# A graph network's isomorphism layer: where the second bias is added and which engine reads the product from PSUM

## The chip, the cores and the metric

The kernel runs on one core of a Trainium2 chip. The metric is the device time of one execution in microseconds (us). The kernel before takes 5115.66 us, the median of 3 runs (5112.63 to 5118.18).

## The reference

Four graph layers follow one another over 100,000 nodes of 64 features and 50,000 edges sorted by destination; each is followed by a residual add and a layer norm. The change touches only the third, the isomorphism layer, which is, for the node table `x` (100,000 x 64):

```
agg = segment_sum(x[src], dst)
h   = relu((x + agg) @ W1 + b1) @ W2 + b2
x   = layernorm(x + (x + relu(h)))
```

W1 and W2 are 64 x 64, b1 and b2 have 64 numbers, all of it in float32.

## The kernel before

The program is a row of passes, one per layer or half layer, each closed by a barrier of all engines: `Sage0`, `Sage1`, `Sage2`, `Gcn1`, `Gcn2`, `Gin` (the isomorphism layer), `Messages`, `Update`. A pass walks over 50 blocks m of 2048 nodes (16 tiles of 128). A block is worked in two groups q = 0, 1 of 8 tiles, so that most operations are instructions of 128 x 512 float32 that come in pairs.

In `Gin` a block goes through these steps; the letters in brackets are the semaphore that each raises.

- GpSimd gathers the source rows of the block's edges, 8 indirect DMAs of 128 rows (`gather_pool`, L678), up to three blocks ahead; it may fill the ring only behind the sums of an older block (`agg0`, `agg1`).
- SyncE copies the gathered rows into three shifted rings, 9 DMAs (`skewed`, L1041), three blocks ahead. The same queue loads the node rows (L864, `load_b`), stores the result (L966) and loads the kept one-hot matrices as bytes (L1103, `bytes`). In one turn m it does, in this order: next index list in every fourth turn (L870); wait for `pre0`, `pre1`, then load_b of m+2; the 9 copies of m+3; wait for `out0`, `out1`, then the store of m; the bytes of m+4. The index list of a turn thus stands right behind the bytes of the turn before.
- TensorE turn m (`tensor`): turn the inputs round (L1225, 8 transposes) once VectorE has made them (`mean`); sums of group 0 of m+1 with one-hot matrices (L749); first product with W1 (L1621); sums of group 1 of m+1; second product with W2 (L1231, 8 matmuls of 128 columns, PSUM banks 6 and 7, `mm`), once ScalarE has made its input (`relu`). In the profile each float32 matmul is two records.
- VectorE turn m (`vector`): inputs of m+1 (`take`, L1550); product plus bias row from PSUM to SBUF (L1559, `sum`); 2x + relu (L1562, `pre`, waits for `last`); row sums, means and centring (L780, L785, L789, `xc`); sums of the squares (L829, `vs`); 1/root (L837) and the result into `store_a` (L843, `out`).
- ScalarE turn m (`scalar`): relu of that sum, SBUF to SBUF (L1598, `last`); turned inputs of m+1 out of PSUM (L1575, `ev`); bytes of m+3 widened to float32 for group 0 (L1128, waits for the DMA of the bytes, `hot0`); squares of m (L810, `sq`); hidden layer of m+1 (L1583, `relu`); roots (L815, `sd`); bytes of m+3 for group 1 (L1128).

The order on each engine is written out by hand; a wait holds up all that stands behind it on its engine.

Of the kernel before, what the change touches and what calls it, by code (L numbers as in the profile page):

```python
# [23 lines left out]
F32, BF16, I32, U8 = mybir.dt.float32, mybir.dt.bfloat16, mybir.dt.int32, mybir.dt.uint8  # L24
ALU = mybir.AluOpType
ACT = mybir.ActivationFunctionType
AX = mybir.AxisListType

P = 128
NT = 16  # L30
BN = P * NT
GT = 8
ET = 8
HT = 4
D = 64
# [28 lines left out]
def build(nc, z, a, out):  # L64
# [5 lines left out]
    def sb(name, shape, dt=F32):  # L70
        return ctx.enter_context(nc.sbuf_tensor(name, shape, dt))
# [14 lines left out]
    def kept(name):  # L86

        return f"{name}_{current[0]}" if name[0:2] == "g_" else name

    def S(name):  # L90
        if name in POOL_DMAS:
            key = kept(name)
            if key not in soft:
                soft[key] = ctx.enter_context(nc.semaphore(key))
            return soft[key]
        if name not in names:
            names[name] = sets[current[0]][len(names)]
        return names[name]
# [28 lines left out]
    def now(uses):  # L127

        return uses + (1 + first[0])

    def before(uses):

        return uses + first[0]
# [20 lines left out]
    def block_of(table, m, width):  # L154
# [20 lines left out]
    wg1, wg2, wi1, wi2 = (sb(n, [P, P]) for n in ("wg1", "wg2", "wi1", "wi2"))  # L175
# [5 lines left out]
    b1r, b2r, bg2r, bi2r, bm2r, bu2r = (  # L181
        sb(n, [P, w]) for n, w in (("b1r", H), ("b2r", D), ("bg2r", D), ("bi2r", D), ("bm2r", D), ("bu2r", D)))
# [3 lines left out]
    ps = [ps_all[:, 512 * i:512 * (i + 1)] for i in range(8)]  # L186

    def work(name, bytes_):
        return sb(name, [P, bytes_ // 4])
# [11 lines left out]
    store_b = [work(f"store_b{u}", NT * H * 4) for u in range(2)]  # L201
    tmp = [[work(f"tmp{k}{q}", 2048) for q in range(2)] for k in range(2)]
    tp = [work(f"tp{q}", 2048) for q in range(2)]
    tq = [work(f"tq{q}", 2048) for q in range(2)]
    stat = sb("stat", [P, 2, 6, GT])
    bytes8 = [sb(f"bytes8_{u}", [P, 2 * HOT], U8) for u in range(2)]
    sq = [work(f"sq{q}", 2048) for q in range(2)]
    ix_now = sb("ix_now", [P, 2 * IX], I32)
    ix_dst = sb("ix_dst", [P, 2 * IX], I32)

# [412 lines left out]
    def bodies(eng, body, by=2, behind=2):  # L623


        n = (NB - behind) // by
        with eng.Fori(0, n) as it:
            for v in range(by):
                body(it * by + v, it * (by // 2) + v // 2, v % 2)
        for m in range(n * by, NB):  # L630
            body(m, m // 2, m % 2)
# [17 lines left out]
    def later(m, i, u):  # L649
        return m + 1, i + u, 1 - u  # L650
# [102 lines left out]
    def group(ap, q, W=D):  # L753

        return ap[:, q * GT * W:(q + 1) * GT * W]

    def tiles3(ap, W=D):
        return ap.rearrange("p (j w) -> p j w", w=W)
# [5 lines left out]
    def row(b, W=D, n=GT):  # L764

        return b[:, :].unsqueeze(1).to_broadcast([P, n, W])
# [8 lines left out]
    def norm_center(ve, m, pre, act_groups=()):  # L775

        V = nc.vector
        for q in range(2):
            ve.wait_ge(S(f"pre{q}"), now(m))
            V.tensor_reduce(stat[:, q, 0, :], tiles3(pre(q)), AX.X, ALU.add).then_inc(S(f"rs{q}"), 1)  # L780
        for q in range(2):
            ve.wait_ge(S(f"rs{q}"), now(m))
            if q in act_groups:
                ve.wait_ge(S(f"shift{q}"), before(m))
            V.tensor_scalar(stat[:, q, 1, :], stat[:, q, 0, :], -1.0 / D, None, ALU.mult).then_inc(S(f"nm{q}"), 1)  # L785
        for q in range(2):
            if q not in act_groups:
                ve.wait_ge(S(f"nm{q}"), now(m))
                V.tensor_tensor(tiles3(tmp[0][q][:, :]), tiles3(pre(q)),  # L789
                                stat[:, q, 1, :].unsqueeze(2).to_broadcast([P, GT, D]), ALU.add).then_inc(S(f"xc{q}"), 1)  # L790
# [40 lines left out]
    def norm_out(ve, m, to, act_groups=()):  # L831
        V = nc.vector
        for q in range(2):
            ve.wait_ge(S(f"sd{q}"), now(m))
            if q in act_groups:
                ve.wait_ge(S(f"out{q}"), before(m))
            V.reciprocal(stat[:, q, 4, :], stat[:, q, 3, :]).then_inc(S(f"rstd{q}"), 1)  # L837
        for q in range(2):
            ve.wait_ge(S(f"rstd{q}"), now(m))
            if q in act_groups:  # L840
                V.tensor_tensor(stat[:, q, 5, :], stat[:, q, 1, :], stat[:, q, 4, :], ALU.mult).then_inc(S(f"shift{q}"), 1)
            else:
                V.tensor_tensor(tiles3(group(to, q)), tiles3(tmp[0][q][:, :]),  # L843
                                stat[:, q, 4, :].unsqueeze(2).to_broadcast([P, GT, D]), ALU.mult).then_inc(S(f"out{q}"), 1)

    class Pass:
# [308 lines left out]
        def vector_loop(self, ve, windows):  # L1155
            for m in range(self.ahead - 1):
                self.hots(ve, m, m, windows)
            self.take_block(ve, 0, 0, 0, windows)
            self.hots(ve, self.ahead - 1, (self.ahead - 1) % 2, windows)
            bodies(ve, lambda m, i, u: self.vector(ve, m, i, u, windows), by=TURN if windows else 2)  # L1160
# [62 lines left out]
    def pair_transposes(pe, src, bank):  # L1223
        for r in range(GT // 2):
            last = pe.transpose(bank[:, r * P:(r + 1) * P], src[:, r * P:(r + 1) * P], ident[:, :])  # L1225
        return last

    def pair_products(pe, lhs, w, bank):

        for r in range(GT // 2):  # L1230
            last = pe.matmul(bank[:, r * P:(r + 1) * P], lhs[:, r * P:(r + 1) * P], w[:, :], start=True, stop=True)  # L1231
        return last

    class Sage2(Pass):
# [228 lines left out]
    class Gcn2(Pass):  # L1463
# [14 lines left out]
        def pre(self, u):  # L1478
            return lambda q: (tmp[1], tq)[u][q][:, :]
# [56 lines left out]
    class Gin(Pass):  # L1536
# [15 lines left out]
        def vector(self, ve, m, i, u, windows):  # L1552
            V = nc.vector
            for q in range(2):
                self.take(ve, *later(m, i, u), q, windows)
            for q in range(2):
                ve.wait_ge(S(f"mm{q}"), now(m))
                ve.wait_ge(S(f"out{q}"), before(m))
                V.tensor_tensor(tiles3(tmp[0][q][:, :]), tiles3(ps[6 + q]), row(bi2r), ALU.add).then_inc(S(f"sum{q}"), 1)  # L1559
            for q in range(2):  # L1560
                ve.wait_ge(S(f"last{q}"), now(m))
                V.scalar_tensor_tensor(tmp[1][q][:, :], group(load_b[u], q), 2.0, tmp[1][q][:, :], ALU.mult, ALU.add).then_inc(S(f"pre{q}"), 1)  # L1562
            norm_center(ve, m, pre_of)
            self.hots_ahead(ve, m, u, windows)
            norm_var(ve, m)
            self.stored(ve, i, u)
            norm_out(ve, m, store_a[u])

        def turned(self, act, m):
            if not exists(m):  # L1570
# [23 lines left out]

        def scalar(self, act, m, i, u, windows):
            for q in range(2):
                act.wait_ge(S(f"sum{q}"), now(m))
                nc.scalar.activation(tmp[1][q][:, :], tmp[0][q][:, :], ACT.Relu).then_inc(S(f"last{q}"), 1)  # L1598
            ahead = m + 3, i + 1 + u, 1 - u
            self.turned(act, m + 1)  # L1600
            self.widen_group(act, *ahead, 0, windows)
            for q in range(2):
                norm_square(act, m, q, pre_of)
            self.bent(act, m + 1)
            norm_root(act, m)
            self.widen_group(act, *ahead, 1, windows)

        def tensor(self, pe, m, i, u, windows):
            if windows:
                places = self.places(m + 1, 0)  # L1610
            for q in range(2):
                pe.wait_ge(S(f"mean{q}"), now(m))
                pe.wait_ge(S(f"ev{q}"), before(m))
                pair_transposes(pe, load_a[q], ps[2 + q]).then_inc(S(f"tr{q}"), 1)
            if windows:
                self.collect(pe, *later(m, i, u), 0, places)
                places = self.places(m + 1, 1)
            for q in range(2):
                pe.wait_ge(S(f"ev{q}"), now(m))
                pe.wait_ge(S(f"relu{q}"), before(m))  # L1620
                pe.matmul(ps[4 + q], wi1[:, :], tp[q][:, :], start=True, stop=True).then_inc(S(f"hid{q}"), 1)  # L1621
            if windows:
                self.collect(pe, *later(m, i, u), 1, places)
            for q in range(2):
                pe.wait_ge(S(f"relu{q}"), now(m))
                pe.wait_ge(S(f"sum{q}"), before(m))
                pair_products(pe, tq[q], wi2, ps[6 + q]).then_inc(S(f"mm{q}"), 1)


    CT = 4  # L1630
# [912 lines left out]
```

## Time and profile before

| | |
|---|---|
| median of 3 runs | 5115.66 us |
| span of the profiled execution, first to last instruction | 5104.4 us |
| mean granted TensorE clock, whole program | 0.937 of full |
| `Gin`, first take to last store | 3419 to 3975 us |
| TensorE, VectorE, ScalarE, GpSimd busy, whole span | 82%, 65%, 54%, 64% |

The profiled execution is told by its span; the work around it has no row of its own, and the span stands 11.3 us below the median of the timed runs. In the timelines a row is: start us, duration us, engine, line, operation, out<-in, how many merged, and in brackets the idle time just before it with what ended it. SPq rows are DMAs as SyncE issues them, not as they move. In the rows by line: busy us and mean ns of one, then the idle time of the engine just before the group.

### The profile page before, as it was taken

To read this page: it belongs to the slowest core of one execution; us is meant where nothing else is said; L and a number is where in the kernel's file an instruction comes from. 1 tells how busy PE (TensorE), PEld (TensorE's weight loads), DVE (VectorE), ACT (ScalarE), POOL (GpSimd) and SP (SyncE) were. 2 spreads that over 40 slices of the span, in tenths; PEclk is the share of its full clock that TensorE was granted. 3 is DMA by queue.
4 is the path that set the end of the run, shared out by engine and by line. 5 is a ranking of instruction groups with operands and counts; after the bars stand their busy time and mean duration, and the time that the engine had idled before them with its cause. 6 is when DMAs were issued, how large, how long until landed. Compare 5 with 4: busy or idle time off the path is not lost. (4 is left out here: it accounts for less than half of the span.)

```text
span 5104.4 us, 115936 instructions
## 1 busy us (share of the span) xinstructions
PE 4188.4 (82%) x31393; PEld 3787.4 (74%) x31394; DVE 3326.6 (65%) x6783; ACT 2761.8 (54%) x7100; POOL 3288.9 (64%) x3162
## 2 busy tenths in 40 slices
PE   2999999799997899979997455548878599999997
PEld 1899999799997898879997454536667366666666
DVE  5555555677775788857676666758888355555555
ACT  0566666455554778754443566656666244444444
POOL 2544443578773777747775777747775677777772
PEclk9999999899999999989999767779999799999999
DMA  1677777466665678758876566657776244444442
GB/s 35 213 252 252 253 251 245 173 233 241 232 235 209 223 258 264 258 198 276 280 265 222 163 186 186 186 148 214 219 210 201 73 121 117 116 117 118 117 115 90
DMA packets 490326, 991.05 MB, mean 194 GB/s; under 512 B 156821, under 2 KB 246965, under 8 KB 470968
## 3 DMA queue, kind: packets, MB, share of 16 engines
q1 hardware_dynamic: 389368, 872.44, 50.6%
q0 software_dynamic: 100800, 116.72, 10.9%
q8 instruction: 72, 1.18, 0.1%
q14 instruction: 86, 0.70, 0.0%
HBM read 452.18 MB, written 380.15 MB: 163 GB/s over the span
## 5 line engine op out<-in xcount | busy, mean ns | idle before, releaser
L749 PE MATMUL ps_all<-arena 128*128 x16000 | 2028.0, 286 | 500.5 <-DMA arena<-arena 365.3
L749 PEld LDWEIGHTS ps_all<-arena 128*128 128x128 f32 x16000 | 1993.3, 204 | 549.1 <-issue 544.7
L678 POOL DMA_INDIRECT arena<-n_t,ix_now x784 | 905.1, 1154 | 429.5 <-issue 404.7
L678 POOL DMA_INDIRECT arena<-y_t,ix_now x784 | 808.3, 1031 | 349.8 <-issue 331.9
L1128 ACT ACTIVATE arena<-bytes 128x2048 f32<-128x2048 uint8 (+1 forms) x300 | 475.9, 1618 | 299.6 <-DMA bytes<-pairs_d 209.2
L678 POOL DMA_INDIRECT arena<-x_rows,ix_now x392 | 373.1, 952 | 375.4 <-PE ps_all L749 263.4
L1639 PE MATMUL ps_all<-w,tp 128*128 128x128 f32 x4000 | 490.9, 276 | 28.8 <-ACT store_b L1782 28.2
L1639 PEld LDWEIGHTS ps_all<-w,tp 128*128 128x128 f32 x4000 | 477.9, 192 | 47.2 <-issue 38.6
L678 POOL DMA_INDIRECT arena<-x_t,ix_now x392 | 385.9, 985 | 191.4 <-issue 172.0
L708 DVE TENSOR_TENSOR arena<-iota,window 128x1024 f32<-128x1024 f32 x302 | 363.4, 1219 | 100.8 <-ACT bytes L1093 93.9
L1093 ACT ACTIVATE bytes<-arena 128x1024 uint8<-128x1024 f32 (+1 forms) x200 | 296.7, 1484 | 241.7 <-DMA pairs_d<-bytes 235.2
L2316 ACT ACTIVATE tp<-ps_all 128x512 f32<-128x512 f32 x298 | 176.6, 593 | 294.9 <-PE ps_all L1634 290.9
L1919 DVE SCALAR_TENSOR_TENSOR tmp<-ps_all,invdeg,load_a 128x128 f32<-128x128 f32 x800 | 225.2, 344 | 161.0 <-PE ps_all L749 127.9
L1739 DVE TENSOR_TENSOR store_a<-ps_all,b1r 128x512 f32<-128x512 f32 x200 | 137.9, 689 | 241.5 <-PE ps_all L1639 222.5
L804 ACT ACTIVATE sq<-tmp 128x64 f32<-128x64 f32 x1200 | 286.8, 245 | 11.3 <-DVE tmp L789 11.3
L2233 POOL DMA_INDIRECT store_a<-x_t,ix_now x200 | 201.3, 1007 | 123.4 <-issue 123.4
L2233 POOL DMA_INDIRECT store_a<-x_t,ix_dst x200 | 214.9, 1075 | 60.9 <-issue 60.9
L2287 DVE TENSOR_TENSOR tmp<-ps_all,bu2r 128x256 f32<-128x256 f32 x200 | 84.9, 424 | 255.4 <-PE ps_all L1639 226.6
L1639 PEld LDWEIGHTS ps_all<-wu,tq 128*128 128x128 f32 x1600 | 202.0, 191 | 51.7 <-issue 47.8
L2233 POOL DMA_INDIRECT store_b<-x_t,ix_now x192 | 198.6, 1034 | 58.5 <-issue 58.5
L703 DVE TENSOR_TENSOR arena<-iota,window 128x2048 f32<-128x2048 f32 x100 | 227.9, 2281 | 10.5 <-PEq L1181 10.5
L804 ACT ACTIVATION_READ_ACCUMULATOR sq<-tmp 128x1 f32 x1200 | 229.8, 191 | 0.0
(204 smaller groups left out, 7653.8 us busy)
## 6 DMA issues: line engine op xcount, KB each, us to landing
x_t<-store_a SPq DMA_DIRECT2D x150, 512.0 KB, 3.1
s_t<-store_a SPq DMA_DIRECT2D x50, 1024.0 KB
n_t<-store_b SPq DMA_DIRECT2D x50, 1024.0 KB
load_a<-s_t SPq DMA_DIRECT2D x50, 1024.0 KB
bytes<-pairs_d SPq DMA_DIRECT2D x100, 512.0 KB
y_t<-store_b SPq DMA_DIRECT2D x100, 512.0 KB, 2.9
load_b<-x_t SPq DMA_DIRECT2D x100, 512.0 KB
arena<-arena SPq DMA_DIRECT2D x147, 192.0 KB
```

The lines of the kernel that those rows point to most:

```text
L678: pool.indirect_dma_start(out=slot_rows(at, W, pitch), out_offset=None, in_=table, in_offset=bass.IndirectOffsetOnAxis(ap=ix_now[:, at:at ...
L703: V.tensor_tensor(hot_matrices(at, q, True), iota[:, :].unsqueeze(1).unsqueeze(1).to_broadcast([P, 2, GT, P]), window[:, 0:2, bass.ds(m * ...
L708: V.tensor_tensor(hot_matrices(at, q), iota[:, :].unsqueeze(1).to_broadcast([P, GT, P]), window[:, 2, bass.ds(m * NT + q * GT, GT)].unsque ...
L749: last = pe.matmul(out(j, 2) if wide else out(j, 1), hot, both(rows) if wide else rows, start=(k == 0), stop=(k == n - 1))
L804: last = A.activation(sq[q][:, j * D:(j + 1) * D], tmp[0][q][:, j * D:(j + 1) * D], ACT.Square, accum_out=stat[:, q, 2, j:j + 1])
L1093: nc.scalar.activation(kept_matrices(u, q, self.two_windows), hot_matrices(self.hot_at(u), q, self.two_windows), ACT.Copy).then_inc(S(f"na ...
L1128: nc.scalar.activation(hot_matrices(self.hot_at(u), q, self.two_windows), kept_matrices(u, q, self.two_windows), ACT.Copy).then_inc(S(f"ho ...
L1639: last = pe.matmul(bank[:, r * P:(r + 1) * P], lhs[:, r * P:(r + 1) * P], w, start=True, stop=True)
L1739: V.tensor_tensor(tiles3(store_a[u][:, c * 512:(c + 1) * 512], H), tiles3(ps[7], H), row(b1r, H, CT), ALU.add).then_inc(S(f"s1{c}"), 1)
L1919: last = nc.vector.scalar_tensor_tensor(tmp[c % 2][q][:, r * P:(r + 1) * P], agg[:, r * P:(r + 1) * P], invdeg[:, bass.ds(m * NT + c * CT ...
L2233: pool.indirect_dma_start(out=self.pairs(v % self.PAIRS, h)[:, to:to + D], out_offset=None, in_=x3_t, in_offset=bass.IndirectOffsetOnAxis( ...
L2316: nc.scalar.activation(tp[s][:, :], ps[2 + s], ACT.Copy).then_inc(S(f"{kind}ev{s}"), 1)
```

## The change

The bias is no longer added by VectorE. Once, at the start of the pass, `bias` splits the bias row into three bf16 parts whose sum is the float32 number, and writes them to partitions 0-31, 32-63 and 64-95 of a 128 x 512 bf16 tile, with zeros below; a second tile of 128 x 128 bf16 holds 1/32 throughout. The scratch lies in `store_b[0]`. Per block and group TensorE first multiplies these two (one bf16 matmul of 512 columns, `start=True`) into bank 6+q and then adds the 4 products of W2 onto it. ScalarE takes the maximum with 0 straight from PSUM; VectorE's instruction from PSUM to SBUF is gone, and with it the semaphore `sum`.

```diff
+    bias_rows = store_b[0][:, 0:256].bitcast(BF16)
+    shares = store_b[0][:, 256:320].bitcast(BF16)
+    bias_part = store_b[0][:, 320:416].bitcast(BF16).rearrange("p (k w) -> p k w", k=3)
+    bias_rest = store_b[0][:, 416:480]
...
-    def pair_products(pe, lhs, w, bank):
+    def pair_products(pe, lhs, w, bank, starts=True):
         for r in range(GT // 2):
-            last = pe.matmul(bank[:, r * P:(r + 1) * P], lhs[:, r * P:(r + 1) * P], w[:, :], start=True, stop=True)
+            last = pe.matmul(bank[:, r * P:(r + 1) * P], lhs[:, r * P:(r + 1) * P], w[:, :], start=starts,
+                             stop=starts or r == GT // 2 - 1)
...
             for q in range(2):
-                ve.wait_ge(S(f"mm{q}"), now(m))
-                ve.wait_ge(S(f"out{q}"), before(m))
-                V.tensor_tensor(tiles3(tmp[0][q][:, :]), tiles3(ps[6 + q]), row(bi2r), ALU.add).then_inc(S(f"sum{q}"), 1)
-            for q in range(2):
                 ve.wait_ge(S(f"last{q}"), now(m))
                 V.scalar_tensor_tensor(tmp[1][q][:, :], group(load_b[u], q), 2.0, tmp[1][q][:, :], ALU.mult, ALU.add).then_inc(S(f"pre{q}"), 1)
+            for q in range(2):
+                ve.wait_ge(S(f"out{q}"), before(m))
...
+        def bias(self, ve):
+            V = nc.vector
+            V.memset(shares[:, :], 1.0 / 32)
+            V.memset(bias_rows[:, :], 0.0).then_inc(S("bias_step"), 1)
+            V.tensor_copy(bias_part[:, 0, :], bi2r[:, :]).then_inc(S("bias_step"), 1)
...
+            for k in range(3):
+                at = slice(k * 32, k * 32 + 32)
+                V.tensor_copy(tiles3(bias_rows[at, :]), bias_part[at, k, :].unsqueeze(1).to_broadcast([32, GT, D])).then_inc(S("bias"), 1)
...
             for q in range(2):
-                act.wait_ge(S(f"sum{q}"), now(m))
-                nc.scalar.activation(tmp[1][q][:, :], tmp[0][q][:, :], ACT.Relu).then_inc(S(f"last{q}"), 1)
+                act.wait_ge(S(f"mm{q}"), now(m))
+                act.wait_ge(S(f"xc{q}"), before(m))
+                nc.scalar.activation(tmp[1][q][:, :], ps[6 + q], ACT.Relu).then_inc(S(f"last{q}"), 1)
...
             for q in range(2):
                 pe.wait_ge(S(f"relu{q}"), now(m))
-                pe.wait_ge(S(f"sum{q}"), before(m))
-                pair_products(pe, tq[q], wi2, ps[6 + q]).then_inc(S(f"mm{q}"), 1)
+                pe.wait_ge(S(f"last{q}"), before(m))
+                pe.wait_ge(S("bias"), now(2))
+                pe.matmul(ps[6 + q], shares[:, :], bias_rows[:, :], start=True, stop=False)
+                pair_products(pe, tq[q], wi2, ps[6 + q], starts=False).then_inc(S(f"mm{q}"), 1)
```

TensorE, end of one turn of `Gin` and start of the next, before (ISA and REGISTER_ALU rows are address arithmetic and semaphores):

```order
L749 MATMUL ps_all<-arena 128x128
L749 ISA
L749 MATMUL ps_all<-arena 128x64
L1231 MATMUL ps_all<-wi,tq 128x128 x8
L730 ISA
L730 TENSOR_LOAD slots
L1225 MATMUL ps_all<-ident,load_a 128x128 x8
```

The same place now:

```order
L753 MATMUL ps_all<-arena 128x128
L753 ISA
L753 MATMUL ps_all<-arena 128x64
L1654 MATMUL ps_all<-store_b 128x512
L1235 MATMUL ps_all<-wi,tq 128x128 x4
L1654 MATMUL ps_all<-store_b 128x512
L1235 MATMUL ps_all<-wi,tq 128x128 x4
L734 ISA
L734 TENSOR_LOAD slots
L1229 MATMUL ps_all<-ident,load_a 128x128 x8
```

Nothing has moved; one matmul (L1654, both operands in `store_b`) stands ahead of each group's four products.

VectorE, one turn of `Gin`, before:

```order
L1550 TENSOR_TENSOR load_a<-ps_all,load_b 128x512 x2
L1559 TENSOR_TENSOR tmp<-ps_all,bi2r 128x512 x2
L1562 SCALAR_TENSOR_TENSOR tmp<-load_b,tmp 128x512 x2
L780 TENSOR_REDUCE stat<-tmp 128x8 x2
```

and now:

```order
L1555 TENSOR_TENSOR load_a<-ps_all,load_b 128x512 x2
L1563 SCALAR_TENSOR_TENSOR tmp<-load_b,tmp 128x512 x2
L784 TENSOR_REDUCE stat<-tmp 128x8 x2
```

The pair between the inputs of the next block and the residual is gone; the residual (now L1563) follows the inputs directly.

## Rows read from the trace of the kernel before

**Rows 1.** Busy time by stretch, columns as its second line names them: the whole pass.

```profile
core 0: us, PE busy (x) PEld busy (x) DVE busy (x) ACT busy (x) POOL busy (x), PEclk, DMA share, GB/s
...
3415.00:3975.00 560.00, 456.82 (x3000) 375.72 (x3000) 457.40 (x900) 339.99 (x596) 368.07 (x374) 0.94 0.68 203
```

**Rows 2.** Waits of the pass, 3430 to 3970: total us, times, longest us.

```profile
ACT tmp L1598 <- DVE tmp L1559: 116.8, 51, 3.3
...
ACT arena L1128 <- DMA bytes<-hot_d: 72.5, 45, 3.8
```

**Rows 3.** The line that begins VectorE's turn: duration ns min/median/max, first and last start.

```profile
L1550 DVE TENSOR_TENSOR load_a<-ps_all,load_b x100: 671/678/692, 3419.0 to 3956.6; 128x512 f32<-128x512 f32 x100
```

**Rows 4.** VectorE's timeline, three turns.

```profile
3605.16 1.28 DVE L1550 TENSOR_TENSOR load_a<-ps_all,load_b 128x512 f32<-128x512 f32 x2
3606.36 1.28 DVE L1559 TENSOR_TENSOR tmp<-ps_all,bi2r 128x512 f32<-128x512 f32 x2
3607.74 1.29 DVE L1562 SCALAR_TENSOR_TENSOR tmp<-load_b,tmp 128x512 f32<-128x512 f32 x2
...
3615.27 1.28 DVE L1550 TENSOR_TENSOR load_a<-ps_all,load_b 128x512 f32<-128x512 f32 x2
...
3626.84 1.28 DVE L1550 TENSOR_TENSOR load_a<-ps_all,load_b 128x512 f32<-128x512 f32 x2
...
3635.41 0.32 DVE L837 RECIPROCAL stat<-stat 128x8 f32<-128x8 f32 x2 [0.73 <-ACT stat L815]
...
3636.93 1.27 DVE L1550 TENSOR_TENSOR load_a<-ps_all,load_b 128x512 f32<-128x512 f32 x2
```

**Rows 5.** SyncE's timeline of the same stretch: DMAs as issued.

```profile
3609.28 0.33 SPq L864 DMA_DIRECT2D load_b<-x_t  x1
3610.30 6.58 SPq L1041 DMA_DIRECT2D arena<-arena  x9
3617.15 0.36 SPq L966 DMA_DIRECT2D x_t<-store_a  x1
3617.84 0.34 SPq L1103 DMA_DIRECT2D bytes<-hot_d  x1
...
3627.85 0.34 SPq L1103 DMA_DIRECT2D bytes<-hot_d  x1
3628.80 0.56 SPq L870 DMA_DIRECT2D ix_now<-src_ix  x1
```

**Rows 6.** ScalarE's timeline of the same stretch.

```profile
3621.85 1.06 ACT L1128 ACTIVATE arena<-bytes 128x1024 f32<-128x1024 uint8 x1 [2.47 <-DMA bytes<-hot_d]
...
3625.38 1.05 ACT L1128 ACTIVATE arena<-bytes 128x1024 f32<-128x1024 uint8 x1
3628.75 1.23 ACT L1598 ACTIVATE tmp<-tmp 128x512 f32<-128x512 f32 x2 [2.33 <-DVE tmp L1559]
...
3631.30 1.06 ACT L1128 ACTIVATE arena<-bytes 128x1024 f32<-128x1024 uint8 x1 [0.35 <-DMA bytes<-hot_d]
```

**Rows 7.** TensorE's timeline, first and last work of one turn.

```profile
3627.58 1.25 PE L1225 MATMUL ps_all<-ident,load_a 128*128 128x128 f32 x8 [0.95 <-DVE load_a L1550]
...
3634.59 2.05 PE L1231 MATMUL ps_all<-wi,tq 128*128 128x128 f32 x16
```

**Rows 8.** Lines of the pass by form, 3430 to 3970.

```profile
L678 POOL DMA_INDIRECT arena<-x_t,ix_now x362 | 357.6, 988 | 134.2 <-issue 114.8 <-PE ps_all L749 18.2 <-DMA arena<-x_t,ix_now 1.2
...
L1231 PE MATMUL ps_all<-wi,tq 128*128 128x128 f32 x788 | 101.2, 282 | 15.5 <-ACT tq L1583 14.6 <-issue 0.7
L1621 PE MATMUL ps_all<-tp,wi 128*128 128x512 f32 x196 | 100.9, 639 | 1.7 <-ACT tp L1575 1.7
...
L1598 ACT ACTIVATE tmp<-tmp 128x512 f32<-128x512 f32 x100 | 61.5, 630 | 116.8 <-DVE tmp L1559 116.8
...
L1575 ACT ACTIVATE tp<-ps_all 128x512 f32<-128x512 f32 x98 | 52.3, 584 | 0.0
```

**Rows 9.** SyncE's timeline in the pass before (`Gcn2`): an index list and what follows.

```profile
3221.05 0.58 SPq L870 DMA_DIRECT2D ix_now<-src_ix  x1
3222.83 6.58 SPq L1041 DMA_DIRECT2D arena<-arena  x9
```

**Rows 10.** The end of VectorE's previous pass and its first instruction in this one.

```profile
3384.21 0.69 DVE L843 TENSOR_TENSOR store_a<-tmp,stat 128x512 f32<-128x512 f32 x1
3419.02 0.69 DVE L1550 TENSOR_TENSOR load_a<-ps_all,load_b 128x512 f32<-128x512 f32 x1 [34.12 <-PE ps_all L749]
```

**Rows 11.** SyncE's own waits, 3430 to 3970.

```profile
SPq L1028 <- DMA arena<-x_t,ix_now: 2.6, 1, 2.6
```

More of the change, by code:

```diff
@@ L1567, in vector, with vector_loop @@
             norm_out(ve, m, store_a[u])
+        def vector_loop(self, ve, windows):
+            self.bias(ve)
+            super().vector_loop(ve, windows)
+        def bias(self, ve):
[3 more added lines that the diff above has]
+            V.tensor_copy(bias_part[:, 0, :], bi2r[:, :]).then_inc(S("bias_step"), 1)
+            ve.wait_ge(S("bias_step"), now(1))
+            V.tensor_tensor(bias_rest[:, :], bi2r[:, :], bias_part[:, 0, :], ALU.subtract).then_inc(S("bias_step"), 1)
+            ve.wait_ge(S("bias_step"), now(2))
+            V.tensor_copy(bias_part[:, 1, :], bias_rest[:, :]).then_inc(S("bias_step"), 1)
+            ve.wait_ge(S("bias_step"), now(3))
+            V.tensor_tensor(bias_part[:, 2, :], bias_rest[:, :], bias_part[:, 1, :], ALU.subtract).then_inc(S("bias_step"), 1)
+            ve.wait_ge(S("bias_step"), now(4))
+            for k in range(3):
+                at = slice(k * 32, k * 32 + 32)
+                V.tensor_copy(tiles3(bias_rows[at, :]), bias_part[at, k, :].unsqueeze(1).to_broadcast([32, GT, D])).then_inc(S("bias"), 1)
         def turned(self, act, m):
```

## The prediction

> **What bounds the kernel now.** Passes are closed by barriers, so only the isomorphism pass counts, and what it gains or loses reaches the end one for one. I read the views in this order: busy time by stretch, waits, then the timelines of four engines over the same two turns. In the stretch nobody is full: TensorE is busy 457 of 560 us, VectorE 457, ScalarE 340 [rows 1]. VectorE's turn begins with the inputs of the next block; these starts run from 3419.0 to 3956.6 for 50 blocks [rows 3], so a turn costs 537.6 / 49 = 10.97 us.
>
> The largest wait in the table is ScalarE's for VectorE's bias add, 116.8 us, and it is the one that the change removes. It is not by itself the bound: ScalarE has slack there. The telling wait is the second, ScalarE's for the DMA that brings the kept one-hot bytes, 72.5 us in 45 waits, nearly every block [rows 2]. The timelines show what that does. Turns alternate: 3615.27 to 3626.84 is 11.57 us, 3626.84 to 3636.93 is 10.09 us [rows 4], 21.66 together.
>
> The long turn is held by a chain through SyncE. VectorE starts the turn at 3605.16, adds the bias at 3606.36, starts the residual at 3607.74 [rows 4]. Only then may SyncE load node rows (3609.28), issue nine ring copies (3610.30, for 6.58 us), store (3617.15) and fetch the bytes (3617.84) [rows 5]. They arrive 4.01 us later: ScalarE begins to widen them at 3621.85 after waiting 2.47 us [rows 6], and behind the widening stand the squares, the hidden layer and the roots, which VectorE needs for its last step; its next turn begins 4.99 us after the widening, at 3626.84. The links are 12.68 + 4.01 + 4.99 = 21.68 us and span two turns (3605.16 to 3626.84), so this loop alone asks for 10.84 us a turn. In the short turn the bytes go out at 3627.85 [rows 5], are widened at 3631.30 after a wait of only 0.35 us [rows 6], and VectorE's own work sets the end, with 0.73 us of idling for the roots [rows 4].
>
> **The change part by part.**
>
> *VectorE's pair of adds goes.* From its start to the residual's start are 3607.74 - 3606.36 = 1.38 us [rows 4]. It stands inside the first link of the loop, once per two turns: 21.68 - 1.38 = 20.30 us, a gain of 0.69 us a turn. It also shortens VectorE's own turn from 10.09 to about 8.7 us, but the loop holds before that: the short turn can shrink only to its own byte wait. Bytes leave about 1.0 us after the turn begins (3627.85 - 3626.84), take 3.45 us, and 4.99 us follow: 9.45 us. The next turn then takes 20.30 - 9.45 = 10.85 us. I count 42 turns in which the loop rules (45 waits [rows 2], less the first ones, in which the rings are still being filled): 42 x 0.69 = 29 us.
>
> *The last turns.* When the blocks with edges have run out, no bytes and no ring copies remain, and VectorE paces. Three turns fall from 10.1 us, as the short one above, to 9.5, where TensorE holds (below), and the tail of the last block loses one pair of adds, 1.3 us: 3 us together.
>
> *ScalarE's relu moves up and reads PSUM.* The pair costs 0.630 us each from SBUF now; the like instruction from PSUM, L1575, costs 0.584 [rows 8]. I price it at no loss. It no longer waits for VectorE, but for TensorE's product, and behind it are queued the turned inputs and the widening. TensorE's product ends at 3634.59 + 2.05 = 3636.64 [rows 7], before VectorE's turn begins at 3636.93 [rows 4]. ScalarE is free by 3625.38 + 1.05 = 3626.43, while its relu starts only at 3628.75 [rows 6]; so it can be done when VectorE comes out of its inputs 1.2 us into the turn. The relu leaves for an idle place, hidden by the inputs' 1.2 us; if that cover goes, the price is the part of the second relu that sticks out, 0.6 us at most.
>
> *TensorE gets two bf16 matmuls of 512 columns a turn.* The trace of before has no such instruction. Below, the nearest row is L1231, 128 columns in float32: 101.2 us / 788 records = 0.128 us a record; above, L1621, 512 columns in float32: 100.9 us / 98 matmuls = 1.03 us each, of two records [rows 8]. It has the width of L1621, so that end is the nearer one, but two-byte numbers where that matmul needs two records of 0.51 us; I expect one record and no more than that, and take 0.3 us, 0.6 us a turn. The Trainium skill, TensorE: Matmul & The Clock Gate, "Wait — 56ns, not 53.3ns?", gives 215.7 ns for 512 bf16 columns back to back at full clock; by that the turn would get 0.43 us. TensorE's own turn, first transpose to last product, is 3636.64 - 3627.58 = 9.06 us [rows 7]. It becomes 9.66 us at most, under the loop's 10.15 us (half of 20.30), and about level with the short turn, whose last 0.2 us the long one then gives back. No time lost. Without that cover, each 0.1 us would cost 5 us over the pass.
>
> *The tables made once at the start.* About ten small VectorE instructions. VectorE stands idle from 3384.9 to 3419.02 [rows 10], waiting for the first sums: nothing.
>
> *What is late next: SyncE and GpSimd.* SyncE's load of node rows now comes at about 1.4 us less, some 2.7 us into the turn. In every fourth turn an index list stands before it: bytes at 3627.85, list at 3628.80 [rows 5], and in the pass before the next DMA came 1.78 us after the list (3221.05 to 3222.83) [rows 9]. That makes 1.01 + 0.95 + 1.4 to 1.8, 3.4 to 3.7 us into the turn, 0.5 us or more too late for the new pace, formerly hidden since the wait for the residual ended at 4.1 us. 11 lists x 0.5 = 6 us lost. GpSimd needs 8 gathers of 0.988 us and a gap of 0.30 us each, 10.3 us a block [rows 8]. That is level with the new pace. It is ahead now: 18.2 us of its idling is waiting for TensorE's sums to free the ring [rows 8], and SyncE's ring copies waited for gathered rows once, 2.6 us [rows 11]. I leave it at nothing, but below 10.3 us a turn there is little more to be had.
>
> Sum: 29 + 3 - 6 = 26 us. The profiled span of 5104.4 us would become 5078; carried to the median of the runs, 11.3 us higher, 5115.7 - 26 = **5090 us**. With the list costing nothing and all 45 turns gaining, 34; with the bytes 0.3 us slower in landing (DMA share now 0.68 [rows 1], higher with shorter turns), 26 - 0.15 x 42 = 20.
>
> **The rivals.**
>
> *The DMAs take it.* If the landing of the bytes lengthens by 1.0 us, from 4.0 to 5.0, since the same bytes must move in less time, the loop gains only 1.38 - 1.0 = 0.38 us in two turns, 8 us over 42 turns less the lists' 6: about 5113 us. For it: the landings of two neighbouring turns differ already, 3.45 and 4.01 us [rows 5, 6]. Against it: a DMA share of 0.68.
>
> *VectorE was the bound.* Then each turn falls to TensorE's 9.66 us: 49 x (10.97 - 9.66) = 64 us at most, and with GpSimd at 10.3 us 49 x 0.67 = 33 us and what its lead allows, some 10 more: about 5073 us. It needs bytes that arrive in under 3.3 us in every turn; against it stand 45 waits. The Trainium skill, DMA: Bandwidth & Descriptors, "Anatomy of one DMA — SWDGE (gpsimd) path", fits a DMA at about 2.0 us plus its bytes over 436 GB/s, an estimate of 2.6 us for these 256 KB; by that rule this rival would hold. The trace disagrees with 3.45 and 4.01 us behind the store and the ring copies on the same queue.
>
> *TensorE becomes the bound (slower).* If a bf16 matmul beside float32 ones costs the float32 price, 1.03 us, the turn is 9.06 + 2.06 = 11.12 us of work, and at the pass's mean granted clock of 0.94 [rows 1] 11.8 us, in front of every second product and of what waits for it: 49 x 0.85 = 42 us slower, 5157 us. It decides from (9.06 + 2b) / 0.94 > 10.97, so b above 0.63 us. Against it: L1621's price is for two records; one is 0.51 us.
>
> *The wait merely changes place.* VectorE could stand before the residual, waiting for the relu, where it used to add the bias. For that the second relu would have to end 1.2 us and more after the turn began; TensorE's product now ends 0.3 us before it, the bias matmuls add 0.6 and the relu 0.6, so 0.9 us. A slower matmul or a second relu held up by the widening before it would close that gap. Time 5106 to 5116.
>
> **How the numbers follow.** A measurement tells about 0.2%, 10 us, from no change. The loop as worked out, 5080 to 5100 us: 0.65. A partial gain of 10 to 16 us (landing slower by half a us): 0.07. VectorE the bound, near 5073: 0.07. DMAs or a new wait take it, within 10 us: 0.14. TensorE the bound: 0.07. So faster 0.79, same 0.14, slower 0.07. The range of 8 in 10 runs from 5076 to 5112 us: it leaves out TensorE's case, most of VectorE's and the last third of the same.
>
> **What the profile after would show.** Right: two blocks take some 20.3 us; ScalarE still waits for the bytes in most turns, now longer than 72.5 us in total, since it arrives there earlier; the wait of 116.8 us for VectorE is gone; the bytes are issued about 11.3 us after the start of the turn before, not 12.7; L1654 adds 0.2 to 0.3 us a group. Wrong: turns under 9.8 us without byte waits (VectorE was the bound); landings of 5 us (the DMAs); idling before L1563 for the relu, or no idling left on TensorE in a turn of 11 us. The forecast falls if L1654 costs over 0.6 us or if GpSimd's gathers turn up as what ends the waits of the ring copies.

## The result and the profile after

The changed kernel takes 5098.52 us (median of 6 runs, 5090.57 to 5104.15) against 5116.39 us of the kernel before in the same session: ratio 0.9965, 95% interval 0.9952 to 0.9977. Measured again in a later session it was 5101.45 against 5108.70 us, ratio 0.9984 (0.9975 to 0.9992). So the change makes the kernel faster by 7 to 18 us, where 26 were forecast. The profiled execution took 5097.06 us around a span of 5095.3. That also corrects a step of mine: 1.8 us lie around the span, not 11.3. If it was so before as well, the profiled execution of before, with a span of 5104.4, took some 5106 us, 10 us less than the median of its runs and less than any of the six. Span against span the change gains 9.1 us: 6.5 between the first and the last turn of the pass, 1.0 ahead of it, 1.5 behind. All comparisons of turns below are with this one fast execution of before, so they are more likely to understate the gain than to overstate it.

The isomorphism pass of the changed kernel, waits from 3430 to 3950, those of SyncE last (total us, times, longest us):

```profile
ACT arena L1132 <- DMA bytes<-hot_d: 147.0, 45, 6.9
...
DVE stat L833 <- ACT sq L814: 104.9, 45, 6.0
...
ACT tmp L1624 <- PE ps_all L1235: 14.1, 29, 1.1
```

```profile
SPq L969 <- DVE store_a L847: 33.8, 17, 6.0
SPq L1032 <- DMA arena<-x_t,ix_now: 27.3, 11, 5.3
SPq L921 <- DVE tmp L1563: 24.8, 26, 3.7
```

The wait of 116.8 us for VectorE [rows 2] is gone, and ScalarE's relu waits 14.1 us for TensorE instead. The wait for the bytes has doubled, from 72.5 to 147.0 us, in the same number of turns (45): ScalarE now arrives earlier at bytes that come little sooner. And SyncE waits for gathered rows 11 times, 27.3 us, where it did so once, 2.6 us [rows 11].

An undisturbed pair of turns, which answers to rows 4 to 7. VectorE and SyncE:

```profile
3603.94 1.27 DVE L1555 TENSOR_TENSOR load_a<-ps_all,load_b 128x512 f32<-128x512 f32 x2
3605.14 1.28 DVE L1563 SCALAR_TENSOR_TENSOR tmp<-load_b,tmp 128x512 f32<-128x512 f32 x2
...
3613.35 1.28 DVE L1555 TENSOR_TENSOR load_a<-ps_all,load_b 128x512 f32<-128x512 f32 x2
...
3624.94 1.28 DVE L1555 TENSOR_TENSOR load_a<-ps_all,load_b 128x512 f32<-128x512 f32 x2
```

```profile
3606.66 0.33 SPq L868 DMA_DIRECT2D load_b<-x_t  x1
3607.68 6.58 SPq L1045 DMA_DIRECT2D arena<-arena  x9
3614.53 0.36 SPq L970 DMA_DIRECT2D x_t<-store_a  x1
3615.22 0.34 SPq L1107 DMA_DIRECT2D bytes<-hot_d  x1
```

ScalarE, and TensorE's new matmul, in the same turns:

```profile
3608.37 1.06 ACT L1132 ACTIVATE arena<-bytes 128x1024 f32<-128x1024 uint8 x1 [1.81 <-DMA bytes<-hot_d]
...
3619.96 1.06 ACT L1132 ACTIVATE arena<-bytes 128x1024 f32<-128x1024 uint8 x1 [3.98 <-DMA bytes<-hot_d]
```

```profile
3602.72 0.38 PE L1654 MATMUL ps_all<-store_b 128*128 128x512 bf16 x1
3602.94 1.05 PE L1235 MATMUL ps_all<-wi,tq 128*128 128x128 f32 x8
```

From the start of the turn to the issue of the bytes, the first link of the loop, are 3615.22 - 3603.94 = 11.28 us, against 12.68 before: the forecast said 11.30. But this is a turn at its best. Over 42 turns the same link measures 12.85 us in the mean before and 12.79 with the change; it is under 11.6 us in 14 of the 42 turns and over 13.6 us in 11. The short turn is 9.41 us (forecast 9.45), the long one 11.59 (forecast 10.85), because the bytes take 3619.96 - 3615.22 = 4.74 us to land, not 4.01 (by landing I mean throughout the time from the issue of the bytes to the start of the widening that waited for them). The third link is 4.98 us, as before. The pair takes 21.00 us, not 20.30.

And a disturbed turn, 3711.11 to 3726.14, 15.03 us long. VectorE's turns, a pause of GpSimd, and SyncE, which loads node rows at 3702.04 and then cannot issue the ring copies:

```profile
3711.11 1.28 DVE L1555 TENSOR_TENSOR load_a<-ps_all,load_b 128x512 f32<-128x512 f32 x2
...
3726.14 1.28 DVE L1555 TENSOR_TENSOR load_a<-ps_all,load_b 128x512 f32<-128x512 f32 x2
```

```profile
3695.17 0.94 POOL L682 DMA_INDIRECT arena<-x_t,ix_now  x1 [3.75 <-issue]
```

```profile
3702.04 0.44 SPq L868 DMA_DIRECT2D load_b<-x_t  x1
3708.38 6.57 SPq L1045 DMA_DIRECT2D arena<-arena  x9
3715.21 0.36 SPq L970 DMA_DIRECT2D x_t<-store_a  x1
3715.90 0.34 SPq L1107 DMA_DIRECT2D bytes<-hot_d  x1
3716.85 0.56 SPq L874 DMA_DIRECT2D ix_now<-src_ix  x1
3717.66 0.38 SPq L868 DMA_DIRECT2D load_b<-x_t  x1
```

Between the load and the first copy lie 6.34 us instead of the 1.02 of the undisturbed turn. TensorE then waits for the copies, and behind that wait its granted clock falls: 0.77 in the mean of this turn (in the rows the third number from the end), against 1.00 in the two turns shown above. The 16 sums take 3.67 us and the first product 3.28 us, against 1.99 and 1.94 us at full clock.

```profile
3716.94 3.67 PE L753 MATMUL ps_all<-arena 128*128 x16 [3.83 <-DMA arena<-arena]
3720.40 3.28 PE L1647 MATMUL ps_all<-tp,wi 128*128 128x512 f32 x4
```

```profile
3711.11:3726.14 15.03, 11.17 (x59) 8.76 (x58) 7.85 (x17) 6.83 (x12) 11.37 (x13) 0.77 0.72 201
3603.94:3613.35 9.41, 8.49 (x60) 7.02 (x60) 7.96 (x17) 6.77 (x12) 7.58 (x7) 1.00 0.75 222
3613.35:3624.94 11.59, 9.53 (x67) 7.71 (x65) 7.86 (x17) 6.85 (x13) 8.84 (x10) 1.00 0.78 228
```

Five turns are longer than 13.5 us after the start-up, all of them at a granted clock of 0.77 to 0.88. Before, two were (13.80 and 13.83 us), both in the start-up, and none after it was over 12.86 us. In the second profile of the change one turn after the start-up is over 13.5 us (13.75).

The three longest waits of SyncE for gathered rows, 4.0, 5.3 and 4.7 us, begin 7 to 9 us behind a pause of GpSimd, of 2.59, 3.75 and 3.04 us, that comes after every 112 gathers. The second profile of the change repeats that (pauses of 2.48, 2.12 and 3.72 us, waits of 4.0, 3.9 and 3.5 us, its three longest after the start-up). The kernel before has the pauses at the same places (4.93, 3.60 and 2.47 us), and SyncE does not wait behind any: there GpSimd's lead covers them.

GpSimd's gathers of the pass, before and after (ns min/median/max, first and last start):

```profile
L678 POOL DMA_INDIRECT arena<-x_t,ix_now x392: 939/945/1445, 3391.6 to 3919.7; - x196
```

```profile
L682 POOL DMA_INDIRECT arena<-x_t,ix_now x392: 940/947/1474, 3389.7 to 3920.1; - x196
```

This is the plainest reading of the case: the gathers take as long as before, 530.4 us against 528.1. What the pass gained, it gained behind the last gather. GpSimd's own pace in the change, 8 gathers of 1.037 us with gaps of 0.30 us, is 10.7 us a block, in a turn of 10.84. VectorE's last turn begins 3949.1 - 3920.1 = 29 us after it, against 3956.6 - 3919.7 = 37 us before: the slack between the gathers and their use was eaten up.

### The profile page after: what moved, and what is told of

Read it like the earlier page. It is cut to its first block and busy times, and to the rows that moved or that the text cites. A ratio compares the mean times of both kernels' runs of the same rounds, so it can differ in the third digit from the quotient of the medians.

```text
span 5095.3 us, 116107 instructions
## 1 busy us (share of the span) xinstructions
PE 4202.0 (82%) x31493; PEld 3798.6 (75%) x31494; DVE 3265.3 (64%) x6692; ACT 2762.0 (54%) x7100; POOL 3310.3 (65%) x3162
## 5 line engine op out<-in xcount | busy, mean ns | idle before, releaser
L682 POOL DMA_INDIRECT arena<-x_t,ix_now x392 | 403.7, 1030 | 176.8 <-issue 166.4
L1235 PE MATMUL ps_all<-wg,tp 128*128 128x128 f32 x1600 | 205.3, 282 | 33.7 <-issue 32.6
```

Of the source, the lines that this page charges most:

```text
L682: pool.indirect_dma_start(out=slot_rows(at, W, pitch), out_offset=None, in_=table, in_offset=bass.IndirectOffsetOnAxis(ap=ix_now[:, at:at ...
```

## The experiments

The twelve runs fall into three sessions, each on one chip. In the first two every kernel with all gathers, the one before too, takes 6308 to 6424 us; there the isomorphism pass costs 13.3 to 13.7 us a turn, and engines idle for spans that the profile does not explain. Only in the third does the kernel before take what it took at first (5108.70 us). I tell it first.

**Half of the gathers left out, kernel before.** `every` is 2 in the isomorphism pass, so 4 of a block's 8 gathers are issued and half of the neighbours' rows are stale; the waits count 4.

```diff
-                for t in range(k * n, k * n + n):
+                for t in range(k * n, k * n + n, every):
...
     class Gin(Pass):
+        every = 2
```

> The kernel before with every second gather of the isomorphism pass left out. With that the change had turns of 10.27 us (503 us from first to last), held by the bytes in 45 waits, though the rest of that program ran at 6245 us. Theory 1 (two turns of the loop hold 1.38 us more before the change): turns of 10.95 us, 535 us from first to last, the ratio to the kernel before 0.978 where the change's was 0.9735. Rival (the loop is not what the removed pair lies in): turns of 10.3 us, ratio 0.9735.

Measured: 5089.38 us, ratio 0.9964 (0.9951 to 0.9977), turns of 10.63 us (520.7 us from first to last). Its waits, 3430 to 3940:

```profile
POOL arena L678 <- PE ps_all L749: 236.3, 81, 7.1
...
ACT arena L1129 <- DMA bytes<-hot_d: 55.7, 46, 1.9
```

GpSimd now waits for TensorE and holds nobody. The forecast of 10.95 us failed: even the kernel before loses 0.34 us a turn to its gathers, not by waits for rows but, for the most part, in the landing of the bytes. Over 44 turns I work out 3.9 us with all gathers and 3.3 us with half; in the turns in which the bytes leave more than 2 us after the turn's start, 4.3 and 3.2. A landing stands once in a loop of two turns, so 0.6 us of it makes 0.3 us a turn.

**Half of the gathers left out, the change.** This one ran in the second session, on one of the slower chips.

> The change, with every second gather of the isomorphism pass left out (4 a block instead of 8, so half of the neighbours' rows are stale). Theory 1: the turns of 13 to 15 us, in which SyncE waits for gathered rows (27.3 us in 11 waits), vanish and the byte loop alone remains, 20.3 to 20.7 us for two turns: 5098 - 24 = 5074. Rival (the missing gain went to slower landings or to TensorE): no more than 5 us faster, 5093 or above.

Measured: 6245.46 against 6423.59 us, ratio 0.9735 (0.9712 to 0.9757). Its total says little beside 5100, since the rest of the program is 25% slower there, but its isomorphism pass runs undisturbed: turns of 10.27 us (503.3 from first to last), no waits of SyncE for rows, no turn over 12.5 us after the start-up, 45 waits for bytes.

```profile
ACT arena L1133 <- DMA bytes<-hot_d: 108.8, 45, 4.9
```

So the turns of 13 to 15 us come with the gathers. The forecast of 20.3 to 20.7 us for two turns holds (20.5). Against before_half_gathers the turn is 0.36 us shorter, 18 us over the pass. That comparison is across two chips, by profiles alone, and the granted clock is not alike in the two: 0.98 over this pass against 0.95, with 4 turns of 43 below full clock against 11. The turns at full clock take 10.11 and 10.38 us in the mean, 0.27 us apart, so the clock has a part in the 0.36. The ratios of the two sessions (0.9735 and 0.9964) may not be set against each other, because the gathers weigh far more on the second chip.

**Pair put back, half of the gathers.** VectorE gets a pair of adds of the same shape, read by nobody, in the place of the removed one; the relu stays early and from PSUM.

```diff
+            for q in range(2):
+                V.tensor_tensor(tiles3(store_b[1][:, q * 512:(q + 1) * 512]), tiles3(group(load_b[u], q)), row(bi2r), ALU.add)
```

> The change with the pair of VectorE instructions put back ahead of the residual, and half of the gathers left out. Theory 1: as before_half_gathers, turns of 10.95 us, ratio 0.978. Rival (what helps is ScalarE's relu that no longer waits for VectorE): as the change with half gathers, 10.27 us and 0.9735.

Measured: 5082.68 us, ratio 0.9952 (0.9939 to 0.9964), turns of 10.50 us. Beside before_half_gathers, on the same chip, that is 0.13 us a turn less; the medians differ by 6.7 us, with intervals that overlap (0.9951 to 0.9964 is in both). Against the change's 10.27, on the other chip, it is 0.23 more. Neither side of the forecast, 10.95 or 10.27, came true. As an estimate the instructions ahead of the residual have two thirds of the 0.36 us and the earlier relu one third; over the turns at full clock (10.38, 10.32 and 10.11 us) it is four fifths and one fifth. The split is not shown more closely than that. The relu's part shows in the short turns: VectorE's own turn is 9.87 us here and 10.02 before, since nothing lies between the pair and the residual any more (1.37 us from the start of the one to the start of the other before, 1.20 here).

**Bytes ahead of the ring copies, half of the gathers, kernel before.**

```diff
                 next_inputs(m + self.inputs_ahead, (u + self.inputs_ahead) % 2)
                 if windows:
+                    if self.skew_late and self.from_kept:
+                        self.load_kept_next(sp, m, u)
                     if self.skew_late:
                         skew()
...
-                if windows:
+                if windows and not (self.skew_late and self.from_kept):
                     self.sync_hot(sp, m, i, u)
```

> The kernel before with half of the gathers left out, and the kept bytes fetched ahead of the nine ring copies. Theory 1: the bytes are out of the loop, their waits vanish, VectorE's own 10.1 us remain: 495 us from first to last, 40 us faster than before_half_gathers, ratio 0.972. Rival (the waits for bytes only mirror another bound): 535 us, 0.978.

Measured: 5093.01 us, ratio 0.9972 (0.9961 to 0.9983), turns of 10.76 us (527.3 us from first to last): no faster than without the edit, rather slower. The waits for bytes are gone altogether, but the forecast of 495 us failed: the bytes are not all that holds the turn. Long turns stay. Two turns, 3611.33 to 3622.14 and 3632.16 to 3644.72, in both of which TensorE waits for the ring copies, until 4.6 and 4.7 us into the turn:

```profile
3615.91 1.99 PE L749 MATMUL ps_all<-arena 128*128 x16 [2.59 <-DMA arena<-arena]
3617.74 1.94 PE L1625 MATMUL ps_all<-tp,wi 128*128 128x512 f32 x4
...
3636.83 2.71 PE L749 MATMUL ps_all<-arena 128*128 x16 [2.68 <-DMA arena<-arena]
3639.33 2.93 PE L1625 MATMUL ps_all<-tp,wi 128*128 128x512 f32 x4
```

```profile
3641.39 0.69 ACT L1587 ACTIVATE tq<-ps_all,bi1c 128x512 f32<-128x512 f32 x1 [2.11 <-PE ps_all L1625]
```

```profile
3611.33:3622.14 10.81, 8.22 (x61) 6.87 (x61) 9.10 (x20) 7.08 (x12) 3.74 (x4) 1.00 0.74 220
...
3632.16:3644.72 12.56, 9.88 (x60) 7.87 (x59) 9.10 (x19) 7.08 (x12) 3.74 (x4) 0.86 0.69 202
```

Behind the wait follow the sums, the first product and the hidden layer, and behind them the roots and VectorE's end of turn. That is a second leg of the loop through SyncE's queue: one leg goes over the bytes and ScalarE's widening, the other over the ring copies and TensorE's sums, and both begin at VectorE's residual. But at full clock a turn with such a wait takes 10.8 us, the first of the two; the further 1.7 us of the second are the clock's: after the wait of 2.68 us TensorE is granted 0.86 of full in the mean of the turn, and the 16 sums and the product take 5.6 us instead of 3.9. It is so in the whole pass. Of 43 turns after the start-up 29 are at full clock and take 10.16 us in the mean, none over 10.87; the other 14 take 11.5 to 13.5 us, 12.16 in the mean. Without the edit 32 turns are at full clock (10.38 us in the mean, none over 10.94) and 11 are below it (11.53). Fetching the bytes early thus did shorten the turns at full clock, by 0.2 us, almost to VectorE's own 10.02. It lost that again where TensorE waited longer for the ring copies (63.9 us in all against 42.5) and its clock fell. The edit itself delays the copies by 0.7 us a turn, so it does not tell what the second leg asks for where they stand first.

**The change itself, once more.**

> The change itself, unaltered, beside the kernel before on a chip like those of the earlier calls, if this call gets one. Theory 1 with GpSimd's gathers as the next bound: where the gathers hold the pass at 13.3 us a turn, the change can give little, 0.996 to 1.000; where the kernel before takes 5116, 0.9965 as in the first measurement.

Measured: 5101.45 us, 0.9984 (0.9975 to 0.9992). Its profile repeats the first one: turns of 10.82 us, 144.1 us of waiting for bytes, and for gathered rows:

```profile
SPq L1032 <- DMA arena<-x_t,ix_now: 21.1, 11, 4.0
```

**The runs on the two slower chips.** Bias by TensorE alone, with VectorE still moving the product (it adds a zero column) and ScalarE's relu behind it:

```diff
-                act.wait_ge(S(f"mm{q}"), now(m))
-                act.wait_ge(S(f"xc{q}"), before(m))
-                nc.scalar.activation(tmp[1][q][:, :], ps[6 + q], ACT.Relu).then_inc(S(f"last{q}"), 1)
+                act.wait_ge(S(f"sum{q}"), now(m))
+                nc.scalar.activation(tmp[1][q][:, :], tmp[0][q][:, :], ACT.Relu).then_inc(S(f"last{q}"), 1)
```

> TensorE multiplies the bias in as in the change, but VectorE still moves the product from PSUM to SBUF (adding a zero) and ScalarE takes the maximum from there, as before. Theory 1 (the loop from VectorE's residual through SyncE's queue to the bytes sets the turn, and the bias matmuls lie in TensorE's idle time): same as before, within 4 us of 5116. Theory 2 (the bias matmuls cost time, which is what is missing of the forecast gain of 26 us): slower than before by 8 us or more.

The relu from PSUM without the bias matmuls:

```diff
-                pe.matmul(ps[6 + q], shares[:, :], bias_rows[:, :], start=True, stop=False)
-                pair_products(pe, tq[q], wi2, ps[6 + q], starts=False).then_inc(S(f"mm{q}"), 1)
+                pair_products(pe, tq[q], wi2, ps[6 + q]).then_inc(S(f"mm{q}"), 1)
```

> The change without the two bias matmuls of a turn; the second bias of the isomorphism layer is left out of the result. Theory 1: as the change, 5098 within 4 us. Theory 2 (the matmuls cost): 5090, the forecast, or less.

The bias matmul three times:

```diff
+                for again in range(2):
+                    pe.matmul(ps[6 + q], shares[:, :], bias_rows[:, :], start=True, stop=True)
                 pe.matmul(ps[6 + q], shares[:, :], bias_rows[:, :], start=True, stop=False)
```

> The change with the bias matmul of each group issued three times instead of once, four matmuls more a turn, about 0.9 us more of TensorE at 0.22 us each. Theory 1 (TensorE has slack in the long turns): at most 10 us slower than the change, 5098 to 5108, by the short turns alone. Theory 2 (TensorE holds the turn): 50 turns by 0.9 us, 45 us slower, 5143.

The pair put back, with all gathers, in both sessions:

> The change, with a pair of VectorE instructions of the removed pair's size put back where it stood; nobody reads their result. ScalarE's relu stays early and from PSUM. Theory 1 (what counts is the 1.38 us ahead of the residual): all of the gain is gone, 5116 within 4 us. Rival (the gain comes from the ScalarE relu that no longer waits for VectorE): the gain stays, 5098.

> Once more the change with a pair of VectorE instructions put back where the bias add stood, since the first call ran where every kernel, that before too, took 6300 us with the isomorphism pass at 13.3 us a turn, held by other waits than those of the theory. Where the kernel before takes about 5116: theory 1 (the 1.38 us ahead of the residual are what counts) says 5116 within 4 us, the rival (ScalarE's earlier relu brings the gain) 5098.

The bytes ahead of the ring copies, in the change and in the kernel before (the edit shown above):

> The change, and SyncE fetches the kept bytes of block m+4 ahead of the nine ring copies instead of behind them and the store. This takes the bytes out of the loop. Theory 1 (bytes first, GpSimd's gathers as the next bound): no waits for bytes, the turn falls from 10.8 to GpSimd's 10.4 to 10.5 us, 15 to 20 us faster than the change: 5080. Rival (TensorE or VectorE hold already): as the change, 5098.

> The kernel before with the bytes fetched ahead of the ring copies. Theory 1: the loop that held its turn at 10.97 us is gone, VectorE's own 10.1 and GpSimd's 10.3 to 10.4 us remain, 5088; the change would then be worth 10 us or less on top. Rival (VectorE was the bound): no gain, 5116.

| kernel | us | kernel before | ratio, 95% interval | turn, us |
|---|---|---|---|---|
| bias by TensorE only | 6307.87 | 6326.69 | 0.9974 (0.9957 to 0.9990) | 13.55 |
| relu from PSUM, no bias | 6308.48 | 6326.69 | 0.9969 (0.9955 to 0.9983) | 13.34 |
| bias matmul three times | 6327.42 | 6326.69 | 1.0003 (0.9985 to 1.0021) | 13.45 |
| pair put back | 6307.64 | 6326.69 | 0.9971 (0.9958 to 0.9985) | 13.26 |
| pair put back, again | 6408.31 | 6423.59 | 0.9978 (0.9963 to 0.9994) | 13.28 |
| change, bytes early | 6416.37 | 6423.59 | 0.9984 (0.9973 to 0.9995) | 13.44 |
| before, bytes early | 6417.75 | 6423.59 | 0.9991 (0.9977 to 1.0006) | 13.70 |

These neither support nor refute the theory where it was meant to hold. In these profiles ScalarE's relu waits for something that the profile can only call remote, and the pass has other bounds; in the first of the two rows below ScalarE, in the second GpSimd, both of the first "pair put back":

```profile
ACT tmp L1626 <- remote: 87.7, 28, 4.3
...
POOL arena L682 <- remote: 56.8, 27, 3.2
```

On their face three of them go against theory 1: the pair put back keeps 0.2 to 0.3%, twice, and so does the bias by TensorE alone, in which VectorE and ScalarE do all that they did before. I have no mechanism for that, and no profile of the kernel before on those chips to look for one; it stays open. The change itself was not measured there with all gathers. What the runs do tell is that bias matmuls are not free there: with six a turn the kernel takes 6327.42 us, with none 6308.48, and with two and the pair put back 6307.64. That is some 19 us for four to six more matmuls a turn, far from the 45 us of a TensorE that holds every turn. Change and kernel before with early bytes differ by 1.4 us there, less than the measurement tells.

## Why the prediction was right or wrong

*What bounds the kernel: half right.* The loop from VectorE's residual through SyncE's queue is there, and short and long turns alternate as said. In an undisturbed turn the first link shrank to 11.28 us, where 11.30 was forecast. But I followed one leg of the loop, over the bytes. The row that would have shown the other, TensorE waiting for the ring copies, was in the same table of waits of before:

```profile
PE ps_all L749 <- DMA arena<-arena: 38.0, 27, 2.6
```

I also took each turn at one clock. In the kernel before 10 of 43 turns are below full clock (0.73 to 0.86) and take 12.12 us in the mean, the other 33 take 10.68; in the change 8 are below it. That is no part of the missing gain, since their number hardly changed, but it makes a turn in which TensorE waits for the ring copies longer than by the wait alone.

*The pair of adds, 42 x 0.69 = 29 us: too much.* Measured are 0.13 and 0.15 us a turn (10.97 to 10.84 and 10.82), 6 to 7 us. This is the step that failed: the first link was to lose 1.38 us in each of 42 turns, and in the mean it lost 0.06 and 0.12 us (12.85 to 12.79 and 12.73). By its parts:

- "What is late next", where GpSimd was put at nothing. The gathers were level with the new pace, 10.3 us a block, and rose above it: from 0.988 to 1.037 us each, 0.4 us a block. The median gather is as long as before (945 and 947 ns), but 74 instead of 36 take over 1.1 us; no run shows why. SyncE's waits for rows went from 2.6 to 27.3 and 21.1 us.
- The landing of the bytes rose from 3.9 us to 4.1 us in both profiles of the change, in the mean of 42 to 44 turns; in the kernel before with half of the gathers it is 3.3, in the change 3.6.
- Even with half of the gathers the change gave 0.36 us a turn, half of 0.69, and the first link lost 0.66 us (12.69 to 12.03), not 1.38. The node rows are loaded 1.1 us earlier, and the store cannot go out before VectorE's result, so part of what SyncE gains it waits away: its waits for the store's result are 8.2 us in before_half_gathers and 23.1 us in change_half_gathers.

*The two rivals of the DMAs and of the moved wait.* "The DMAs take it" foretold 5113 with landings of 5 us; they rose by 0.2 us, not 1.0, so a small part of it happened. "The wait merely changes place" did not: VectorE waited 0.9 us for the relu in 96 instructions.

*The bias matmul, 0.3 us each: 0.22 us* from its start to that of the product behind it (3602.72 to 3602.94; the two records overlap). The Trainium skill, TensorE: Matmul & The Clock Gate, "Wait — 56ns, not 53.3ns?", gives 215.7 ns for it, and that row agrees. The rival in which TensorE holds, from 0.63 us on, was never near.

*The tables at the start: nothing,* as forecast. *ScalarE's relu from PSUM:* 0.593 us against 0.630. *The index lists, 6 us lost: not tested.* The list at 3716.85 is followed by the load at 3717.66, 0.81 us, not 1.4 to 1.8; the gap in the pass before [rows 9] held a wait of SyncE for gathered rows. Still, the load comes 0.5 us later in the 11 turns with a list (median 3.22 against 2.73 us into the turn), as forecast. No run takes the lists out, so what that costs is not shown.

*The last turns:* with the blocks' edges gone, the last turn is 8.63 us, not 9.5: TensorE's 9.66 us included sums that no longer run.

*The rival in which VectorE was the bound* did not come: 45 waits for bytes stayed. The rule that stands beside it in the prediction (the Trainium skill, DMA: Bandwidth & Descriptors, "Anatomy of one DMA — SWDGE (gpsimd) path") is a fit of DMAs that GpSimd issues. SyncE issues these bytes, so it was no estimate for them.

*The time.* The range 5076 to 5112 held both measurements; the gain was 0.3 to 0.7 of the forecast. The prediction also named a sign by which it would fall, gathers as what ends the waits of the ring copies, and that sign came, 11 times. That the range held owes something to luck: the reasons for which it reached up to 5112 (slower landings by half a us, a wait that merely moves) are not the ones that took the gain.

## What to carry to other kernels

A wait that a change removes is worth what the next loop leaves of it. Before counting the gain, list for each engine and queue its own work per turn, with the gaps between its instructions: here GpSimd, busy for 368 of 560 us, stood at 10.3 us a block, level with a turn that was to go from 10.97 to 10.28, and its pauses were covered only as long as it was ahead. Where a loop runs through a DMA queue, follow all transfers behind the same wait. And read the granted clock turn by turn before a long turn is put down to a wait: here the same wait made a turn of 10.8 us at full clock and one of 12.6 us at 0.86.

## What the hardware showed that I had not expected

With eight gathers a block the bytes land later than with four: 4.3 us against 3.2 where they leave more than 2 us into the turn, though the gathers' queue took only 11.3% of the DMA engines' time and the queue of the plain DMAs 59.6% (kernel before, 3430 to 3950). GpSimd pauses ahead of the 113th, 225th and 337th gather of the pass, after every 14 blocks, for 2.1 to 4.9 us, at the same places in the kernel before and in both profiles of the change, and no row says for what. TensorE's granted clock falls to half mostly around waits of 1.5 to 4 us for the ring copies, but not at every such wait: in before_early_half it stayed full behind one of 2.59 us and fell behind one of 2.68. And the same kernel takes 5109 us in one session and 6327 or 6424 us in the two others, at a mean granted TensorE clock of about 0.935, 0.866 and 0.858; each session had another chip, and whether it is the chip that differs is not shown.
